# Attention products with the values: two tiles back to back in every second tile instead of one in each

## What is computed

```python
mod = (_silu(L0_c) @ L0_wmod).reshape(L0_c.shape[0], 6, 1, -1)   # sa, ca, ga, sb, cb, gb
h = _layernorm(x) * (1 + ca) + sa
qkv = h @ W_qkv.T + b_qkv                      # q, k, v: (2, 16 heads, 2048, 16)
logits = jnp.einsum('bhqd,bhkd->bhqk', q, k) / jnp.sqrt(jnp.float32(HEAD))
logits = jnp.where(causal[None, None], logits, -jnp.inf)
attn = jax.nn.softmax(logits, axis=-1)
o = jnp.einsum('bhqk,bhkd->bhqd', attn, v)
x = x + ga * (o.reshape(...) @ W_out.T + b_out)
x = x + gb * ffn(_layernorm(x) * (1 + cb) + sb)
```

## Time and profile before

| | |
|---|---|
| median of 3 runs | 1410.3 us (1407.01 to 1412.68) |
| the profiled execution: its own time | 1412.92 us |
| its span | 1411.2 us |
| TensorE's matmuls busy | 1300.2 us (92%) |
| VectorE busy | 1032.8 us (73%) |
| ScalarE busy | 774.5 us (55%) |
| attention stage, first values to last, about | 857 us (205 to 1062) |

### The profile page before, as it was taken

The page is one execution under the profiler, slowest core; times in us unless marked ns, Lnnn a source line. Parts: engine busy times, 40 slices in busy tenths (PEclk is TensorE's granted clock), DMA queues, the critical chain, the costliest instruction groups (busy, mean ns, idle before and its releaser), DMA issues. The chain is left out here.

```text
span 1411.2 us, 26070 instructions
## 1 busy us (share of the span) xinstructions
PE 1300.2 (92%) x8566; PEld 693.9 (49%) x8566; DVE 1032.8 (73%) x1862; ACT 774.5 (55%) x1009; POOL 172.8 (12%) x101
## 2 busy tenths in 40 slices
PE   4983899999999999999998999999999899999997
PEld 3873233343333333333333334334326788888886
DVE  4893988888888778788787788888822566666663
ACT  2762046666666556566665666666681444454442
POOL 1468300000000000000000000000001212332221
PEclk8997589999999999999999999999999999999998
DMA  6444230021021011003003002000004001222200
GB/s 205 134 163 155 75 100 16 17 61 32 18 59 35 18 42 54 17 9 83 17 5 78 17 18 64 7 6 10 5 6 129 11 23 40 59 59 59 59 15 30
DMA packets 75813, 71.09 MB, mean 50 GB/s; under 512 B 17816, under 2 KB 68704, under 8 KB 75688
## 3 DMA queue, kind: packets, MB, share of 16 engines
q1 hardware_dynamic: 75688, 69.51, 17.9%
HBM read 47.57 MB, written 21.23 MB: 49 GB/s over the span
## 5 line engine op out<-in xcount | busy, mean ns | idle before, releaser
L862 DVE TENSOR_REDUCE mx<-ps 128x1 f32<-128x512 f32 (+3 forms) x1120 | 701.4, 671 | 152.5 <-PE ps L732 76.1
L816 ACT ACTIVATE prob<-ps 128x1024 f32<-128x1024 f32 (+3 forms) x640 | 547.8, 895 | 364.9 <-PE ps L760 222.1
L729 PE MATMUL ps<-kst,qst 96*128 96x512 bf16 (+3 forms) x1280 | 421.5, 362 | 25.0 <-DMA kst<-qk_parts 22.5
L756 PE MATMUL ps<-qst,kst 99*128 99x512 bf16 (+3 forms) x1280 | 358.8, 350 | 7.0 <-issue 6.1
L772 PE MATMUL ps<-prob,vw 128*32 128x512 f32 (+3 forms) x2560 | 300.6, 542 | 0.0
L729 PEld LDWEIGHTS ps<-kst,qst 96*128 96x128 bf16 x1280 | 121.4, 98 | 334.0 <-DVE mx L862 234.3
L756 PEld LDWEIGHTS ps<-qst,kst 99*128 99x128 bf16 x1280 | 119.2, 99 | 105.4 <-ACT prob L816 20.3
L760 PE MATMUL ps<-mask_k,ident_bf 128*128 128x128 bf16 x512 | 103.7, 222 | 0.0
L732 PE MATMUL ps<-mask_q,ident_bf 128*128 128x128 bf16 x512 | 102.9, 227 | 0.0
L772 PEld LDWEIGHTS ps<-prob,vw 128*32 128x32 f32 x2560 | 50.4, 108 | 105.3 <-issue 75.9
L935 POOL COPY vw<-v_nat 128x1024 f32 (+1 forms) x8 | 8.3, 1044 | 703.6 <-PE ps L772 703.5
(11 more groups left out here) (148 smaller groups left out, 1379.2 us busy)
## 6 DMA issues: line engine op xcount, KB each, us to landing
qk_parts<-parts SPq DMA_DIRECT2D x32, 384.0 KB, 3.0
qst<-qk_parts SPq DMA_DIRECT2D x192, 64.0 KB, 2.6
kst<-qk_parts SPq DMA_DIRECT2D x192, 64.0 KB, 2.5
xs<-in_x SPq DMA_DIRECT2D x16, 512.0 KB, 6.4
o_rows<-o_sb SPq DMA_DIRECT2D x128, 32.0 KB, 1.7
o_raw<-o_rows SPq DMA_DIRECT2D x16, 256.0 KB
rd<-rden_rows SPq DMA_DIRECT2D x16, 256.0 KB
out<-y SPq DMA_DIRECT2D x8, 512.0 KB, 3.2
```

What stands on the lines that cost most here:

```text
L729: last = pe.matmul(at, qst[gc][0:QK_ROWS, J, h0 + h, i % 4 * P:(i % 4 + 1) * P], kst[gc][0:QK_ROWS, cb, h0 + h, 0:width], start=True, stop ...
L756: last = pe.matmul(ps[:, h, 0:width], kst[c][0:ST_ROWS, t // 4, h, t % 4 * P:(t % 4 + 1) * P], qst[c][0:ST_ROWS, J, h, skip:BLK], start=Tr ...
L816: act.activation(prob[:, n % P_BUFS, 2 * pair:2 * pair + 2, 0:width], ps[:, 2 * pair:2 * pair + 2, 0:width], ACT.Exp).then_inc(exp_done, 1)
L862: dve.tensor_reduce(mx[:, h0:h0 + nh, i % 4, cb], ps[:, bank, 0:nh * width].rearrange("p (h x) -> p h x", h=nh), AX, ALU.max).then_inc(max ...
```

## The change

In even tiles no values are multiplied. In each odd tile n, at the same place of the tile (behind `logits(n, 0)` and the tile's first slot of maxima), the values of tiles n - 3 and n - 2 are multiplied one directly behind the other. Odd tiles' values stay where they were, those of even tiles come one tile later. The number of instructions is the same, and so are the queues of the other engines. What stands behind the last tile of the last step is not changed.

```diff
@@ -781,10 +781,12 @@
                 for n in range(NKT):
                     logits(n, 0)
                     maxima(SLOTS_OF_TILE * n)
-                    if n >= PV_LAG:
-                        values(n - PV_LAG, s, c)
-                    elif not (isinstance(s, int) and s == 0):
-                        values(NKT + n - PV_LAG, s - 1, 1 - c)
+                    if n % 2 == 1:
+                        for m in (n - 1 - PV_LAG, n - PV_LAG):
+                            if m >= 0:
+                                values(m, s, c)
+                            elif not (isinstance(s, int) and s == 0):
+                                values(NKT + m, s - 1, 1 - c)
                     maxima(SLOTS_OF_TILE * n + 1)
                     logits(n, 1)
                     maxima(SLOTS_OF_TILE * n + 2)
```

## The result

| | before | changed |
|---|---|---|
| median | 1410.3 us | 1438.2 us (1437.6 to 1439.7, 3 runs) |
| ratio, 95% interval | | 1.0205 (1.0177 to 1.0234) |
| span of the profiled execution | 1411.2 us | 1436.5 us |
| VectorE busy, ScalarE busy | 1032.8, 774.5 us | 1013.2, 769.7 us |

The changed kernel is slower by 2.0%: 28 us by the medians, 25.3 us by the spans. The forecast was 1436, slower.

The account below looks back on a forecast made before the run. TensorE's queue, in its written order, was taken to set the time; -30 + 24 + 5 + 21 + 6 = +26 us on the median of 1410.3 gave 1436 us, own range 1420 to 1450, 1410 to 1452 with rival 2.

Parts of the forecast that it names:

- joins: Values of two tiles multiplied back to back on TensorE: 159 times 0.19 us saved, 30 us (14 to 37).
- turns: Transposes of the maxima in tiles 24, 32, 4 and 20: without values ahead, TensorE waits longer, +21 us.
- wide and narrow cycles: Two-tile stretches: 90 with 512-wide logits wait 0.27 us each, +24 us; 63 narrower ones 0.08, +5 us.
- end of the last step: Last step's end, without units: logits wait 1.08 us for exponentials in 6 two-tile stretches, +6 us.
- behind another V, a V should cost its two pitches, 0.90: On TensorE, a product with the values directly behind another costs 0.90 us, without entry, saving 0.19.
- The one that was followed: Tiles 27 to 29: two tiles take 5.50 us, 5.47 before, with TensorE waiting 0.22 for an exponential.
- on the edge: In tiles 27 to 29, a unit arrives at 1.74 us, just when VectorE frees its bank.
- the first (only the drain counts): Rival: TensorE's two-tile stretches find banks free after all, so 30 us are gained: 1380; chance 0.08.
- The second (waits that stand in for one another): Rival: half of the waits at wide two-tile stretches and transposes vanish (22 us), +4: 1414; chance 0.12.
- The third (VectorE runs dry beyond what was counted): Rival: VectorE starves during paired values; some 140 two-tile stretches lose another 0.15 us, +21: 1457; chance 0.08.
- VectorE's and ScalarE's busy times: Sign of being right: in the profile after, both engines' busy times unchanged, with their idle time up.
- the second V starts 0.88 behind the first: Sign: second product with the values starts 0.90 us behind the first if right, 1.00 or more if wrong.

Follow-up runs that it names:

- end_only: The kernel before, with products with the values paired only in tiles 25 to 39 of the last step: 1417.0 us, ratio 1.0049.
- no_21: The changed kernel with only the pair of values in tile 21 undone, so tile 20 keeps its values ahead of the transpose: 1425.3 us.
- pad: The kernel before, no pairs, with one more VectorE instruction (a memset) ahead of the transpose in tile 20: 1422.0 us.
- act_after: The changed kernel with ScalarE's exponentials over half of the columns (first eight tiles of step 0 whole) and the exponent scaled by 0.01: 1419.6 us.

## Why the prediction was right, and where its terms were off

The direction, the mechanism and the total were right: 26 us forecast from the sum, 28 measured by the medians and 26.4 in the ledger. That the total came so near is in part luck, since terms that were off by up to some 12 us lie on opposite sides. Term by term:

| term | forecast, us | ledger, us |
|---|---|---|
| joins | -30 | -37 |
| turns | +21 | +18.8 |
| wide and narrow cycles | +24 and +5 | 19.4 + 13.4 - 7.8 = +25.0 |
| end of the last step | +6 | +7.8 (from `end_only`) |
| clock | none | +12.5 |
| loop's back edge | none | -0.5 |

*Joins.* The step "behind another V, a V should cost its two pitches, 0.90" was too dear: the fours in a pair start 0.45, 0.43 and 0.43 apart, so only the first half of the first product pays 0.03 more than its columns. A join saves 0.23, the upper of the two bounds that were given (all of the fixed part goes), instead of 0.19. The Trainium skill, TensorEngine Tiling (Array Packing), section Key Properties, says that a change of tiling mode drains the engine. The trace agrees: the cost comes once for each change of mode, and the column of values halves with the number of changes. V is also the only product in fp32 there, and no run separates the two. The transpose, which is bf16 and 48 columns wide, speaks against the type, though it is an operation of another kind: the logits behind it start 829.53 - 829.38 = 0.15 later, 0.05 of which are its columns, so leaving it costs 0.10 as well.

*Turns.* Tile 24: forecast 0.66 more, measured 1.37 - 0.69 = 0.68. Tile 20: 0.49 forecast, 0.41 measured. Tile 32: 1.05 forecast, 0.88 measured. There the missing part stands just ahead of the turn: L1(32) waits for an exponential, 0.19 us behind the end of the unit ahead of it, and what TensorE loses there it doesn't lose again at the transpose. The two together are 1.07.

```profile
849.55 0.59 PE L729 MATMUL ps<-kst,qst 96*128 96x512 bf16 x2
...
850.17 0.11 PEld L756 LDWEIGHTS ps<-qst,kst 99*128 99x128 bf16 x2 [0.35 <-ACT prob L818]
```

*Cycles.* The one that was followed came out at 5.46 us for 5.50, with 0.22 of waits for 0.22, though not quite as written: 0.14 are the exponential's and 0.08 VectorE's, which the forecast had put "on the edge". Over all cycles VectorE's part is larger than forecast (13.4 us at units, where 5 stood for the narrow ones) and ScalarE's smaller (11.6 in the middle of the stage, where 24 stood). That the sum came to 25 for 29 hides that each of the two was off by a factor of two or more.

*Clock.* This is the missing term. The forecast looked at each wait as a length and took the clock to stay at 1.00, as in the earlier trace rows. `no_21` and `pad` show what it overlooked: at the turn in tile 20, 0.4 us more of wait brings the lower clock behind it in most steps. The total came out right because this omission (12.5 us) and the joins' undervalued gain (7 us) lie on opposite sides, and because the rest, taken together, erred by 5 us. Without the clock the changed kernel would have been slower by about 1%, not 2%.

Of the rivals, the first (only the drain counts) is what happens when the other engines are quick, and only then: -25.6 us with both halved. The second (waits that stand in for one another) is seen in parts, as at tile 32, but not at half: of 50 us of waits at cycles and turns, 44 came. The third (VectorE runs dry beyond what was counted) is seen in part: the waits of units grew by 13.4 us where 5 were forecast, 8 of the 21 that this rival had added. Of the signs, VectorE's and ScalarE's busy times did not stay, as said above; the second V starts 0.88 behind the first, for 0.90.

## What to carry to other kernels

Grouping work of one kind on a saturated engine saves the cost of changing over, but it also gathers the pauses in which the other engines catch up; count how many buffers lie between them, follow one cycle with starts and ends from the trace, and compare the wait that it finds with the cost that is saved. Look first at the places where the engine already waits: what stood ahead of such a place was filling it, and a wait made longer can cost more than its length if the clock falls behind it. The cheapest gain here was the reverse of the change, moving a piece of work into an existing wait.

## What the runs showed of the hardware that was not expected

- The granted clock fell from its 2.4 GHz to its 1.2 GHz level behind a wait of TensorE of 1.94 to 1.99 us in 7 of 8 steps of the changed kernel and 3 of 8 of `act_after`, and of 2.03 to 2.07 us in `pad` in 6 of 8, in streams that are otherwise dense; behind waits of 1.53 to 1.58 us at the same place it stayed up in all 8 steps. The price was 1 to 2 us each time. The Trainium skill, in TensorE: Matmul & The Clock Gate, section Part 1: The HAM clock gate, describes two such levels, with the lower one when the engine was idle; the trace agrees with the two levels.
- Products in 32-column tiles directly behind one another cost next to nothing beyond their columns: half a product of 512 columns in fp32 takes 0.43 us, and twice 512 columns at 2.4 GHz are 0.427. Entering and leaving this mode costs 0.10 and 0.12 us.
